# Weights summed in two chains on GpSimd, keys made in column tiles of 32, first loads and zeros placed differently, and a new order of ticks, in an attention and experts kernel on one core

## What is computed

```python
x = x + xattn(layernorm(x), ctx, ctx, ...)   # 16 batches of 128 rows, 512 wide; ctx has 2048 rows
x = x + attn(layernorm(x), Ww, Wr, ...)      # a delta rule in chunks of 64 rows, 4 heads of 128
x = x + ffn(layernorm(x), Wg, w1, w2)        # top-1 routing to 16 experts, 512 -> 2048 -> 512, relu
# xattn: 16 query heads of 32 share one key head and one value head of 32
Q = (q @ Wq + bq); K = k @ Wk + bk; V = v @ Wv + bv
attn = softmax(Q K^T * scale); out = attn V; return out @ Wo + bo
```

## Time and profile before

| what | value |
|---|---|
| median of 3 executions | 2082.02 us (2079.54 to 2087.32) |
| the profiled execution, its own time | 2085.92 us |
| its span, first to last instruction | 2084.1 us |
| PE busy | 2006.0 us, 96% |
| POOL busy | 1642.0 us, 79% |
| DVE / ACT busy | 1274.3 / 1101.0 us |
| mean granted clock of PE | 0.977 |

### The profile page before, as it was taken

The page is one execution under the profiler, slowest core; times in us unless marked ns, Lnnn a source line. Parts: engine busy times, 40 slices in busy tenths (PEclk is TensorE's granted clock), DMA queues, the critical chain, the costliest instruction groups (busy, mean ns, idle before and its releaser), DMA issues. The chain is left out here.

```text
span 2084.1 us, 33310 instructions
## 1 busy us (share of the span) xinstructions
PE 2006.0 (96%) x11884; PEld 1316.3 (63%) x11884; DVE 1274.3 (61%) x2218; ACT 1101.0 (53%) x2029; POOL 1642.0 (79%) x1387
## 2 busy tenths in 40 slices
PE   7779999999999999999999999999999899999998
PEld 4335565656565555556555656555555889999998
DVE  5656777776776777776777777777762333333333
ACT  2555565656566656656565656665553143333333
POOL 1778999999999999998999999999896055555555
PEclk7789999999999999999999999999998999999999
DMA  6752131212121221312121212221200199999994
GB/s 225 212 133 62 57 106 46 77 47 76 59 65 66 67 69 54 100 37 95 44 77 44 77 66 57 68 64 24 96 1 17 66 377 354 352 352 355 357 357 172
DMA packets 105125, 262.16 MB, mean 126 GB/s; under 512 B 8576, under 2 KB 33920, under 8 KB 96256
## 3 DMA queue, kind: packets, MB, share of 16 engines
q1 hardware_dynamic: 96912, 234.92, 32.8%
q10 hardware_dynamic: 4464, 14.62, 2.4%
q0 software_dynamic: 3584, 10.49, 1.3%
HBM read 223.67 MB, written 25.72 MB: 120 GB/s over the span
## 5 line engine op out<-in xcount | busy, mean ns | idle before, releaser
L1041 POOL TENSOR_TENSOR psum<-psum,weights 128x512 f32<-128x512 f32 x896 | 1155.6, 1290 | 113.4 <-ACT weights L665 6.6
L835 DVE TENSOR_REDUCE mpart<-bank 128x1 f32<-128x512 f32 x1024 | 677.0, 685 | 353.9 <-PE bank L420 349.2
L665 ACT ACTIVATE weights<-bank 128x512 f32<-128x512 f32 x1024 | 589.1, 596 | 379.9 <-PE bank L433 363.6
L433 PE MATMUL bank<-qT,kT 97*128 97x512 f32 x1024 | 498.5, 494 | 20.9 <-DMA qT<-mrow 13.5
L420 PE MATMUL bank<-kT,qT 96*128 96x512 f32 x1024 | 431.4, 440 | 9.9 <-DVE mpart L835 5.2
L433 PEld LDWEIGHTS bank<-qT,kT 97*128 97x128 f32 x1024 | 193.8, 192 | 192.9 <-issue 102.6
L420 PEld LDWEIGHTS bank<-kT,qT 96*128 96x128 f32 x1024 | 198.4, 194 | 144.2 <-DVE mpart L835 73.1
L445 PE MATMUL bank<-weights,v 128*32 128x512 f32 x2048 | 267.5, 618 | 0.0
L1293 POOL TENSOR_TENSOR w2l<-w,w2h 128x1024 fp32r<-128x1024 f32 x64 | 202.0, 3157 | 78.0 <-PE ebank L1206 57.0
L1236 ACT ACTIVATE hh<-ebank 128x512 fp32r<-128x512 f32 x64 | 38.3, 598 | 226.6 <-PE ebank L1190 226.6
L1230 ACT CAST w2h<-w 128x2048 fp32r<-128x2048 f32 x64 | 121.5, 1898 | 43.1 <-DMA w<-in_w 43.1
(11 more groups left out here) (168 smaller groups left out, 2803.4 us busy)
## 6 DMA issues: line engine op xcount, KB each, us to landing
w<-in_w SPq DMA_DIRECT2D x48, 2048.0 KB, 20.1
w_first<-in_ctx SPq DMA_DIRECT2D x64, 1024.0 KB, 5.0
w_first<-in_w SPq DMA_DIRECT2D x16, 2048.0 KB, 12.0
dispatched<-route ACTq DMA_DIRECT2D x17, 513.0 KB, 8.9
dis<-dispatched SPq DMA_DIRECT2D x16, 513.0 KB, 3.5
qT<-qh SPq DMA_DIRECT2D x128, 64.0 KB, 2.1
qT<-qs SPq DMA_DIRECT2D x64, 64.0 KB, 2.1
xr<-in_x SPq DMA_DIRECT2D x16, 256.0 KB, 2.7
```

The costliest lines, as they stand in the source:

```text
L433: e.matmul(B_BANK[u % 2][:], kT[b % 2][0:3 * HD + 1, k * P:(k + 1) * P], qT[b % 2][0:3 * HD + 1, g * 512:(g + 1) * 512], start=True, stop= ...
L665: e.activation(p[n % NP], B_BANK[u % 2][:], ACT.Exp).then_inc(p_act.sem, 1)
L835: e.tensor_reduce(mpart[g % 2][:, 4 * (n % 4) + n // 4:4 * (n % 4) + n // 4 + 1], max_bank(b, g, n)[:], AX.X, ALU.max).then_inc(max_dve.se ...
L1041: e.tensor_tensor(acc[:], first, p[(UNITS * b + u) % NP], ALU.add).then_inc(psum_pool.sem, 1)
```

## The change

- `add_weights` keeps two sums for each group: even blocks go to `psum`, odd blocks to a new buffer `podd`. Both start at their second block, and a last add joins them: 15 adds as before.
- `prepare` on PE makes each 64 columns of keys and values as two matmuls of 32 columns.
- ACT's copy goes straight to `kvs` (`kvlow` is gone), DVE adds into it, and some waits move from DVE to ACT.
- First loads: SP loads identity, wq, ctx 1 to 3; ACT's queue bias, x, wkv, ctx 0. For batch 0, one of the three parts of the queries is sent from ACT's queue.
- Zeros go out every 12 ticks over iterations 0 and 1; the waits for them move to DVE's x2 and to POOL's indirect transfer of batch 0.
- All tick tables are new.

```diff
-STEADY = Prep(norm=-59, norm_pool=-59, xn=-29, xnt=15, xnt_act=21, qproj=[24, 26, 28, 31], q_dve=30, q_act=55,
-              q_pool=55, qsend=58, kv=[18, 42, 55, 70], kvlow=[18, 42, 55, 74], kvs=[20, 52, 67, 75], ...
+STEADY = Prep(norm=-53, norm_pool=-32, xn=14, xnt=21, xnt_act=30, qproj=[38, 41, 45, 47], q_dve=45, q_act=47,
+              q_pool=50, qsend=58, kv=[25, 51, 64, 77], kvlow=[27, 52, 65, 78], kvs=[27, 58, 74, 99], ...
-FIRST = Prep(norm=4, norm_pool=4, xn=6, xnt=12, xnt_act=8, qproj=[12, 13, 14, 17], q_dve=15, q_act=16, q_pool=18,
-             qsend=19, kv=[10, 26, 43, 48], ...
+FIRST = Prep(norm=4, norm_pool=4, xn=6, xnt=8, xnt_act=8, qproj=[11, 12, 13, 40], q_dve=15, q_act=16, q_pool=18,
+             qsend=19, kv=[7, 10, 40, 62], ...
-LOAD_AFTER, W1_AT = 4, 80
+LOAD_AFTER, W1_AT, ZERO_AT, ZERO_STEP = 4, 80, 34, 12
-PE_AT = dict(sums=11, x1=[18, 19, 20, 22], ..., I=46, X1=50, Vn=100, oT2=103,
+PE_AT = dict(sums=14, x1=[28, 29, 30, 31], ..., I=48, X1=51, Vn=100, oT2=104,
-POOL_AT = dict(xb=4, norm2=22, x12=25, rn=30, MT0=40, XT1=42, norm3=113, row=136)
+POOL_AT = dict(xb=4, norm2=25, x12=25, rn=30, MT0=39, XT1=39, norm3=114, row=136)
...
-            return 15 * g + max(k, 1) - 1
+            return 15 * g + (k - 2 if k >= 2 else k)
...
             e.dma_start(ident, T["consts"][:, C_IDENT, :]).then_inc(ident_in.sem, 16)
-            for c in range(4):
+            weight(e, wq[:], "Wq").then_inc(wq_in.sem, 16)
+            for c in (1, 2, 3):
                 load_ctx(0, c)
...
                     for j in range(DC):
-                        rows = slice(64 * (j % 2), 64 * (j % 2) + 2 * HD)
-                        ins = e.matmul(KV_BANK[rows, :], wkv[:, j, :], cxT[c][:, j, :], start=j < 2, stop=j >= 2)
+                        for n in (0, HD):
+                            row = 2 * HD * (j % 2) + n
+                            ins = e.matmul(KV_BANK[row:row + HD, :], wkv[:, j, n:n + HD], cxT[c][:, j, :],
+                                           start=j < 2, stop=j >= 2)
...
+            e.dma_start(bias[:], T["bias"]).then_inc(bias_in.sem, 16)
+            e.dma_start(xin[:], T["x"][0]).then_inc(x_in.sem, 16)
             e.dma_start(wkv[:], T["Wkv"]).then_inc(wkv_in.sem, 16)
-            e.dma_start(xin[:], T["x"][0]).then_inc(x_in.sem, 16)
-            e.dma_start(bias[:], T["bias"]).then_inc(bias_in.sem, 16)
-            weight(e, wq[:], "Wq").then_inc(wq_in.sem, 16)
+            e.dma_start(cxT[0], T["ctx"][0, 0]).then_inc(ctx_in[0].sem, 16)
...
                     e.copy(qh[:], qs[:]).then_inc(q_act.sem, 1)
+                    if b == 0:
+                        e.wait_ge(*q_act.at(0))
+                        for h in range(4):
+                            send_part(e, 0, 1, qh, h).then_inc(q_in.sem, 16)
...
-                    if b or c:
-                        e.wait_ge(*(kvs_dve.at(b, c - 1) if c else kvs_dve.at(b - 1, 3)))
-                    e.copy(kvlow[half(c), :], KV_BANK[half(c + 1), :]).then_inc(kvlow_act.sem, 1)
+                    if b and c % 2 == 0:
+                        e.wait_ge(*vT_pe.at(b - 1, c // 2))
+                        e.wait_ge(*kl_dve.at(b - 1, c + 1))
+                    e.copy(kvs[c // 2][half(c), :], KV_BANK[half(c + 1), :]).then_inc(kvlow_act.sem, 1)
...
-                if t >= 34 and t % 4 == 2 and (t - 34) // 4 < ZEROES:
+                if t >= ZERO_AT and (t - ZERO_AT) % ZERO_STEP == 0 and (t - ZERO_AT) // ZERO_STEP < ZEROES:
...
-                if k == 0:
+                if k < 2:
                     return
+                n = HG * b + g
+                acc = podd if k % 2 else psum[n % 5]
                 e.wait_ge(*p_act.at(b, u))
...
+                elif k == 3:
+                    if n:
+                        e.wait_ge(*psum_pool.at(0, 15 * n - 1))
                 else:
-                    e.wait_ge(*psum_pool.at(b, 15 * g + k - 2))
-                    first = acc[:]
+                    e.wait_ge(*psum_pool.at(b, 15 * g + k - 4))
+                first = acc[:] if k >= 4 else p[(UNITS * b + u - 2) % NP]
                 e.tensor_tensor(acc[:], first, p[(UNITS * b + u) % NP], ALU.add).then_inc(psum_pool.sem, 1)
+                if k == KB - 1:
+                    e.wait_ge(*psum_pool.at(b, 15 * g + 13))
+                    e.tensor_tensor(psum[n % 5][:], psum[n % 5][:], podd[:], ALU.add).then_inc(psum_pool.sem, 1)
```

More of the change, by code:

```diff
@@ new lines @@
+LOAD_AFTER, W1_AT, ZERO_AT, ZERO_STEP = 4, 80, 34, 12
+PE_AT = dict(sums=14, x1=[28, 29, 30, 31], xn2T=38, V=[41, 42, 43, 44], rkT=46, I=48, X1=51, Vn=100, oT2=104,
+             x2=[108, 109, 110, 111], xn3T=121, lg=124, loc=134, Y=[55, 62, 72, 81, 88, 97], Z=[56, 65, 76, 82, 92,
+             98], XT=[61, 68, 77, 87, 96])
+ACT_AT = dict(xn2=34, ss=37, rk=43, xn2T=37, V=45, rkT=46, X1=50, Vn=100, oT2=104, xn3=119, xn3T=121, eg=126, X=[58,
+              69, 77, 84, 92])
+DVE_AT = dict(recip=[10, 12, 14, 15], att=24, x1=35, XT1=45, MT=46, IT=47, x2=110, lg=124, oh=127, row=136, Y=[54,
+              59, 71, 77, 86, 94], Z=[54, 62, 74, 80, 89, 100])
@@ L71 @@
+MAX_DVE = [-39, -39, -35, -34, -28, -28, -27, -26, -25, -25, -22, -22, -21, -19, -10, -10]
+MAX_TURN, MAX_ROW, PV_AT = -7, -8, [18, 24, 33, 35]
+O_COPY = 10
+FIRST_MAX, FIRST_TURN = [63, 63, 63, 67, 79, 79, 80, 80, 80, 91, 111, 111, 113, 114, 116, 116], 116
 class Count:
@@ L160, in attention @@
         cxT = [w1_first[:, c, :].rearrange("p (c t) -> p c t", c=DC) for c in range(4)]
-        kvlow, kvs = sb("kvlow", [P, 512]), [sb(f"kvs{i}", [P, 512]) for i in range(2)]
+        kvs = [sb(f"kvs{i}", [P, 512]) for i in range(2)]
         v1 = [sb(f"v1{i}", [P, KB, HD]) for i in range(2)]
@@ L309, in weight, with send_part @@
             return e.dma_start(dst, T[src])
+        def send_part(e, b, part, src, h):
+            return e.dma_start(
+                qT[b % 2][part * HD:(part + 1) * HD, :].bitcast(F32).rearrange(
+                    "d (g h t) -> d g h t", g=HG, h=4)[:, :, h, :],
+                src[h * HD:(h + 1) * HD, :].bitcast(F32).rearrange("d (g t) -> d g t", g=HG))
         @block.sync
@@ L336, in send_queries @@
                 for part, src, ready in ((0, qh, q_act), (1, qh, q_act), (2, qs, q_pool)):
[L337 to L343, removed]
+                    if b or part != 1:
+                        e.wait_ge(*ready.at(b))
+                        for h in range(4):
+                            send_part(e, b, part, src, h).then_inc(q_in.sem, 16)
             for i in range(-2, B + 2):
@@ L815, in _ @@
                         finish(i - 1, t)
-                    if i == 0:
-                        once(t)
+                    if i in (0, 1):
+                        once(TICKS * i + t)
         @block.vector
@@ L863, in prepare @@
                     e.wait_ge(*kvlow_act.at(b, c))
-                    if b and c % 2 == 0:
-                        e.wait_ge(*vT_pe.at(b - 1, c // 2))
-                        e.wait_ge(*kh_act.at(b - 1, 2 * c + 3))
-                        e.wait_ge(*kl_dve.at(b - 1, c + 1))
                     e.scalar_tensor_tensor(kvs[c // 2][half(c), :], KV_BANK[half(c), :], bkv[half(c), :],
-                                           kvlow[half(c), :], ALU.add, ALU.add).then_inc(kvs_dve.sem, 1)
+                                           kvs[c // 2][half(c), :], ALU.add, ALU.add).then_inc(kvs_dve.sem, 1)
                 if t in prep(b).kl:
@@ L940, in finish @@
                         e.wait_ge(*scat_out.at(b - 1))
+                    else:
+                        e.wait_ge(*zeroed.at(ZEROES - 1))
                     e.tensor_tensor(x2, P_BANK[:], x12[:], ALU.add).then_inc(late_dve.sem, 1)
```

32 lines of the change are left out of this document (13 added, 19 removed).

## The result

The changed kernel takes 2046.03 us (median of 4 runs, 2043.38 to 2050.84) against 2080.78 (2078.36 to 2087.32) on the same chip: a ratio of 0.9824, with a 95% interval of 0.9807 to 0.984. It is faster by 35 us. The forecast was 86 us faster, and the result lies 1 us above the range of 1960 to 2045 us.

What follows compares the result with a forecast made beforehand. It took POOL to be full at 95.5 us per steady iteration, with PE at 89. Gains of 63 + 13 + 7 + 3 + 0 = 86 us gave 1999.9 profiled, 1996 us median; range 1960 to 2045.

Steps and rivals of the forecast that it cites:

- What bounds the kernel: Steady iteration: POOL is full at 95.5 us and sets the period; PE has 89 us of work.
- PE's need: PE's work per steady iteration, summed from starts of single matmuls: 89.8, taken as 89 us, with about 6 us hidden idle.
- The 91: Forecast steady iteration in us, 2 above PE's work, down from 95.5; ends 91 and 95.5.
- A: Rival: PE's hidden idle stays as latencies of chains, so PE needs 93.5 us per iteration; 2034 us; chance 0.13.
- the steady window: Sign in the steady iterations: 91 us expected; staying above 94 would show the prediction wrong.
- the first product for a maximum: Sign at the first loads: first maximum near 30 us, against 32.65 before.
- Part 1: Two sums on POOL: 7.5 us of gaps gone per iteration, 4.5 us gained in each of iterations 2 to 15, 63 us.
- Part 2: New tick tables: sums move from tick 11 to 14, no more instructions; priced inside the 91 us iteration.
- Part 3: Keys and values on PE in column tiles of 32: taken at 0, near ends -10 and +8 us.
- Rival D: Keys and values on PE: halves do not run side by side, a piece takes 3.74 us; 2136 us; chance 0.06.
- Part 4: Zeros spread out: 13 us gained in iteration 0 (ends 5 and 18), 7 in iteration 1 (ends 0 and 10).
- Part 5: First loads, sends moved from SP's to ACT's queue: 3 us gained, ends -3 and 6.

Runs made afterwards that it cites:

- four waits: Kernel of before with two sums and copy straight to kvs, old ticks; four adds of each second group wait for the add before: 2051.28 us (0.9828).
- even waits: Changed kernel in which every second add (blocks 4, 6, ..., 14) waits for the add just before it: 2055.44 us (0.9867).

## Why the prediction was wrong

The steps in the order of the prediction.

**What bounds the kernel.** That POOL set the period of before, with 0.18 us lost at each dependent add, was right as far as it goes: its busy time and gaps fill the 95.5 us, and the two sums alone, once four waits let DVE in, bring the period to 94.2. But PE's own need lay 2.8 us below the 95.5 (92.7, in the new order), and not 6.5. The kernel with one sum under the new ticks (100.0 us) is no measure of the gaps, since PE's standstill and its low clock are in it. The Trainium skill ("GPSIMD Engine Reference", Instruction dispatch) says that an instruction's completion holds back what waits on its semaphore and not the next instruction of POOL; the trace agrees, with gaps of 0.14 us in one case and none in the other.

**PE's need.** This is the step that failed. It put "some 89 of real work" in the place of PE's busy time, from the starts of single matmuls, and the runs show 92.7. The 89 left out what PE loses when it goes into a group of column tiles and comes out of it, 0.09 to 0.1 us each time, an estimated 3.5 us per iteration. The prediction had the sign of it in hand: eight short matmuls took 0.98 ahead of a weigh group, and it took 0.11 for each "as the 0.98 holds a change of shape". The change was taken off there and counted nowhere. Rounding the sum of 89.8 down to 89 added 0.8, and the other terms were together some 0.6 too high. The busy time of 94.3 that was set aside was the better bound. The 91 was therefore below the floor: at 92.7 the most that an iteration could give against 95.5 was 2.8, where 4.5 was forecast, and 1.3 came in most. Of the rivals A named the right cause only in part. It forecast 93.5 per iteration and 2034 us from chains of latency; the floor is PE's own work, and waits for POOL and DVE are the 1.5 us above it. The low end of the range was also a slip: the steady part at 90 and -10 of the tiles make 1972 and not 1960, and A with the tiles at +8 makes 2042 at the other end. Of the signs that the prediction named, the steady window stayed above 94, which was to show it wrong, and the first product for a maximum started at 37.63 us, not near 30.

**Part 1.** The step asked what waits for the gaps to go away and not who used them. A gap in POOL's adds was a chance for DVE to read its two operands. The Trainium skill ("GPSIMD Engine Reference", Specifications) says that the SBUF interfaces are shared with VectorE, with contention for DVE instructions in a two-port mode or with two inputs in SBUF. The traces agree and give it a size, 7.57 us for an instruction of 0.68. It turns the two sums under the old order from a gain into a loss of 3.7%, and iteration 0 of the changed kernel takes 93.7 us where it takes 82.1 with one sum and 85.1 with waits on every second add. 63 us was forecast for parts 1 and 2 together, and 28 came.

**Part 2, new ticks.** Priced inside part 1. In the steady part they give nothing that four waits under the old ticks do not give: both have 94.2. With two sums and no waits they are worth 8.2 us per iteration; the second subtraction takes 2.4 us in their order and 7.6 in the old one. With one sum they cost 4.5 (100.0 against 95.5), with PE's standstill and the low clock in it.

**Part 3, tiles of 32.** Priced at 0, right for a piece: 1.86 against 1.87. Rival D, which forecast 3.74, is ruled out. The estimate from the overhead per matmul of the Trainium skill ("TensorEngine Tiling (Array Packing)", Instruction Overhead), 13 us more, is not seen in a piece either; what that section advises against is to tile along a dimension that is already small, and it gives no price for two column tiles in place of one. Whether the tiles cost the 0.5 us per iteration that tiles of 64 gain, by when DVE meets POOL, stays open.

**Part 4, zeros.** 13 forecast for iteration 0 and 7 for the next; 7.6 and 4.3 came. The mechanism was right: waits for the row of maxima fell from 14.6 to 2.6 us. Iteration 0 gave part of it back to the subtraction of 7.75 us: it takes 85.1 with the even waits and 93.7 without.

**Part 5, first loads.** The sign was wrong: 6.6 us lost to the first score where 3 were to be gained. The step counted SP's issue time and not which transfer PE's first instruction needs. The first piece of ctx was moved behind three others in ACT's queue while wq and three pieces went out on SP's, and PE could start on it at 15.65 us, where before it had started at 7.45.

## What to carry to other kernels

Before a gap on an engine is closed, ask who works in it: here the gaps of 0.14 us between POOL's adds let a DVE instruction with two operands in SBUF through, and four waits put back gave 112 us. A sum of single starts leaves out what lies between kinds of work: here 0.1 us at each way into and out of column tiles, 36 times in an iteration. Check such a sum against a run in which the other engines are relieved. Where parts of a change are judged, try them under both orders; each of these two halves alone was slower than either kernel.

## What was not expected of the hardware

A DVE subtraction of 32 x 512 with both operands in SBUF took 0.68 us alone and up to 7.75 beside POOL's adds without gaps in the changed kernel, 8.79 in the one with the maxima halved. Each one of more than 5 us ended some 0.55 us after the POOL instruction ahead of the first gap, also when that gap was 0.08 us long. Others went in without a gap (the 1.20 us at 323.41).

PE's granted clock in the steady windows was 1.00 where PE was filled. It was 0.96 with one sum under the new ticks, 0.96 with the products halved, and 0.97 with two sums under the old ticks. In each of these three PE stood once in an iteration, for 2.8, 3.5 and 6.2 us, and a stretch of 6.8 us or more at 1.2 GHz began during the standstill or within 2 us of its end. The changed kernel stands for 1.0 us once in an iteration and keeps 2.4 GHz; in the kernel of before the clock fell twice behind a standstill of 0.65 us. So with less work for PE an iteration became longer, 95.7 against 94.2 us; the standstill behind the subtraction and the low clock both lie in it.

Going from matmuls of 128 columns into a group of column tiles, and coming out again, cost PE 0.09 to 0.1 us each way.
